# Weight preparation moved: transposes between the edge tables' counts, the experts' split beside the second feed-forward

## The reference, cut to what matters

```python
xn = layernorm(x)
x = x + gcn(xn, W, edges) + mix0(xn)             # message sum over the edges; attention mixer; feed-forward 0
x = x + experts0(layernorm(x))                   # 8 experts
xn = layernorm(x)
x = x + attention(xn, src, dst, Wq, Wk, Wv, Wp)  # edge softmax, then: h = layernorm(...)
                                                 # h = gelu(h @ W1.T + b1) @ W2.T + b2     (feed-forward 1)
    + ball_mixer(xn, w_qkv, w_dw, w_pw, w_res)   # convolution weights
x = x + shared(layernorm(x)) + top2_of_8(layernorm(x), W1p, W2p)
```

## Time and profile before

| what | value |
|---|---|
| median of 3 runs | 3988.4 us (3985.86 to 3989.91) |
| the profiled execution | 3987.43 us, span 3985.7 us |
| TensorE busy | 2587.3 us (65% of the span) |
| VectorE busy | 2170.5 us (54%) |
| ScalarE busy | 1269.1 us (32%) |
| GpSimd busy | 1315.5 us (33%) |
| mean granted TensorE clock | 0.807 |

### The profile page before, as it was taken

One profiled execution on the slowest core, in us unless ns is written; L12 is line 12 of the kernel. 1 busy time (PEld: TensorE's weight loads), 2 busy tenths in 40 slices (PEclk: granted clock), 3 DMA queues, 4 the chain that ended last, 5 costly groups with the idle time before them and its releaser, 6 DMA issues. The chain is left out here.

```text
span 3985.7 us, 66521 instructions
## 1 busy us (share of the span) xinstructions
PE 2587.3 (65%) x17122; PEld 2086.2 (52%) x17123; DVE 2170.5 (54%) x4408; ACT 1269.1 (32%) x2467; POOL 1315.5 (33%) x1017
## 2 busy tenths in 40 slices
PE   4413333436678699996375434777777487699997
PEld 4413333323367477774254423555555366589986
DVE  6523333322456388885237764777777555544445
ACT  0300010003143255553257732222222243345441
POOL 0048888853000000000001024888888500211115
PEclk9855555557679599997597767999999778699998
DMA  1046666730000000001200015777777200356643
GB/s 36 32 105 157 156 165 162 197 94 6 0 22 0 16 11 13 16 16 46 73 0 0 0 40 150 193 189 187 189 191 189 52 21 0 124 188 229 227 159 91
DMA packets 255391, 373.00 MB, mean 94 GB/s; under 512 B 119009, under 2 KB 180889, under 8 KB 250965
## 3 DMA queue, kind: packets, MB, share of 16 engines
q0 software_dynamic: 154752, 174.53, 18.2%
q1 hardware_dynamic: 87700, 185.50, 14.2%
q10 hardware_dynamic: 12864, 12.06, 1.1%
HBM read 320.09 MB, written 50.96 MB: 93 GB/s over the span
## 5 line engine op out<-in xcount | busy, mean ns | idle before, releaser
L750 POOL DMA_INDIRECT ms_got<-gather,ms_index x400 | 506.2, 1265 | 124.9 <-issue 114.4
L1689 POOL DMA_INDIRECT as_gkv<-gather_kv,as_index x340 | 462.0, 1359 | 108.7 <-issue 100.9
L811 PE MATMUL ms_total<-ms_got,ms_hot 125*125 125x256 f16 x1040 | 231.0, 410 | 376.8 <-DMA ms_got<-gather,ms_index 251.9
L811 PEld LDWEIGHTS ms_total<-ms_got,ms_hot 125*125 x1040 | 202.9, 219 | 405.0 <-issue 405.0
L2097 POOL MEMSET bm_fx<- 128x128 f32 x1 | 0.2, 205 | 1013.0 <-POOLq L115 1013.0
L1810 PE MATMUL as_total<-as_gkv,as_hot 125*125 125x264 f32 x850 | 218.8, 406 | 78.0 <-DVE as_summed L555 65.6
L1478 ACT ACTIVATE ex_h<-ex_up,ex_now 128x313 f32<-128x313 f32 (+1 forms) x320 | 196.1, 613 | 197.2 <-PE ex_up L458 190.0
L1810 PEld LDWEIGHTS as_total<-as_gkv,as_hot 125*125 125x125 f32 x850 | 157.7, 193 | 117.8 <-issue 91.8
L2791 DVE CAST moe_hidden<-moe_h 128x256 f16<-128x256 f32 (+1 forms) x336 | 101.8, 303 | 209.9 <-ACT moe_h L2728 209.3
L2728 ACT ACTIVATE moe_h<-moe_up,moe_w 128x256 f32<-128x256 f32 (+1 forms) x336 | 163.1, 487 | 135.2 <-PE moe_up L458 93.2
L1784 PE MATMUL as_picked<-y_rows,as_pick 125*125 x1060 | 150.3, 291 | 52.6 <-issue 47.7
(11 more groups left out here) (448 smaller groups left out, 5895.2 us busy)
## 6 DMA issues: line engine op xcount, KB each, us to landing
moe_w<-wsplit SPq DMA_DIRECT2D x34, 2052.0 KB
as_dsts<-in_dst SPq DMA_DIRECT2D x83, 305.2 KB
wsplit<-ms_split SPq DMA_DIRECT2D x36, 512.0 KB
ms_raw<-in_L_ffn_W1p SPq DMA_DIRECT2D x16, 512.0 KB
ms_raw<-in_L_ffn_W2p SPq DMA_DIRECT2D x16, 512.0 KB
results<-moe_made SPq DMA_DIRECT2D x32, 256.0 KB, 8.2
ms_got<-gather,ms_index POOLq DMA_INDIRECT x400
gather_kv<-qkv_out SPq DMA_DIRECT2D x5, 1250.0 KB
```

Source lines behind the costliest of these rows:

```text
L750: pool.indirect_dma_start(out=got[:, s, j, :], out_offset=None, in_=m.gather0, in_offset=bass.IndirectOffsetOnAxis(ap=index[:, s, j:j + 1] ...
L811: ins = pe.matmul(total[:, visit % RING, 0:C], hot[:, visit % RING, j, :], got[:, s, j, p * C:(p + 1) * C], start=(j + p == 0), stop=(j + ...
L1689: pool.indirect_dma_start(out=gkv[s][:, j, 0:2 * C], out_offset=None, in_=m.gather_kv, in_offset=bass.IndirectOffsetOnAxis(ap=index[:, s, ...
```

## The change

`Turner` is moved in front of `edge_tables` and used there: its 26 blocks are spread over the 20 steps of the counts, which are written out instead of looped, and ScalarE's loads, copies and stores stand before its one square root. The `Splitter` is used in `feed_forward("ff1")`, with four steps in each of the first four chunks and two in the last; its `high` stand on ScalarE behind gelu 3 and 11 and, twice, behind gelu 15; its `low` on VectorE behind units 7 and 15 and behind additions 2 and 4. The message sum keeps neither. `feed_forward` loses the code for more than one expert, which no call used. The core of the diff:

```diff
 def edge_tables(nc, m, a, src, dst):
...
+        turner = Turner(nc, m, a, ph)
...
             @block.scalar
             def _(act):
+                for i in range(2):
+                    turner.load(act, i)
+                turner.store(act)
                 act.wait_ge(s_span, 2)
                 act.activation(m.degree_s[:, 0, :], m.degree_s[:, 0, :], ACT.Sqrt).then_inc(s_rows, 1)
+                turner.finish(act)
...
+                steps, blocks = ET // SET, len(turner.blocks)
+                for i in range(steps):
+                    pe.wait_ge(s_hot, i + 1)
+                    add(i % 2, i == 0, i == steps - 1)
+                    turner.turn(pe, range(blocks * i // steps, blocks * (i + 1) // steps))
...
 def message_sum(nc, m, a):
...
-        turner = Turner(nc, m, a, ph)
-        splitter = Splitter(nc, m, a, ph)
...
-                        if splits and s % 2:
-                            splitter.low(dve, i, s // 2)
...
-                    turner.turn(pe, part, PARTS)
...
+def feed_forward(nc, m, a, name, W1, b1, W2, gain, bias_in, splits=False):
+    PIECES = 4
...
+                if splits:
+                    with sp.Fori(0, X8) as e:
+                        for h in range(2):
+                            splitter.move(sp, e, h)
+                    for h in range(2):
+                        splitter.move(sp, X8, h)
+                    splitter.finish(sp)
...
+                def highs(c, own, k):
+                    if splits and (own or k < 2):
+                        for s in range(2):
+                            splitter.high(act, c * PIECES + k, s)
+                def chunk(c, own):
+                    for u in range(units):
...
+                        act.activation(h32[:, u % 4, 0:n], up[:, u % 4, 0:n], ACT.Gelu,
+                                       scale=1.0 / WS, bias=bias[:, f:f + 1]).then_inc(s_h32, 1)
+                        if u % 8 == 3:
+                            highs(c, own, u // 8)
+                    highs(c, own, 2)
+                    highs(c, own, 3)
...
+                def chunk(c, own):
+                    for u in range(units):
...
+                        if u % 8 == 7:
+                            lows(c, own, u // 8)
+                    for j in range(J):
...
+                        if j in (2, 4):
+                            lows(c, own, 1 + j // 2)
```

More of the change, by code:

```diff
@@ L565, in finish @@
         self.dve.sem_inc(s_pace, 1)
[L568 to L625, removed]
@@ L762, in _ @@
                 adder = Adder(nc, dve, "ms", m.x, total, s_total, s_added, m.inv_sqrt_degree)
-                def groups(i, splits):
+                with dve.Fori(0, G // SLOTS) as i:
                     for s in range(SLOTS):
@@ L784, in groups @@
                         dve.tensor_copy(index[:, free, :], nxt).then_inc(s_index, 1)
-                        if splits and s % 2:
-                            splitter.low(dve, i, s // 2)
-                    return before + count
-                with dve.Fori(0, whole) as i:
-                    groups(i, True)
-                with dve.Fori(whole, G // SLOTS) as i:
-                    visits = groups(i, False)
-                adder.finish(dve.snap(visits), s_pace)
+                adder.finish(dve.snap(before + count), s_pace)
             @block.tensor
@@ L906, in feed_forward, with part, every_chunk @@
             ph.sem(x) for x in ("up", "h32", "hhigh", "hidden", "down", "added"))
-        ph.ahead(s_h32, s_hidden, s_down, s_added)
+        splitter = Splitter(nc, m, a, ph) if splits else None
+        if splits:
+            splitter.s_pace = s_pace
+        ph.ahead(s_hidden, s_down, s_added, s_h32)
         units = FB * len(HALVES)
         w1_32 = w[:, 0:CB * F].rearrange("p (b n) -> p b n", b=CB)
-        def part(s, k, layer, b, at, n):
+        def part(k, layer, b, at, n):
             start = b * F + at if layer == 0 else CB * F + b * C + at
-            return w16[:, s, k, start:start + n]
+            return w16[:, k, start:start + n]
+        def every_chunk(eng, work):
+            with eng.Fori(0, CHUNKS - 1) as c:
+                work(c, True)
+            work(CHUNKS - 1, False)
         with nc.Block() as block:
@@ L919, in _ @@
             def _(sp):
[L920 to L933 removed]
+                sp.dma_start(w1_32, W1.rearrange("(b p) n -> p b n", p=128)).then_inc(s_w, 16)
@@ L1008, in _ @@
+                every_chunk(act, chunk)
             @block.vector
             def _(dve):
[L1010 to L1012 removed]
+                dve.tensor_scalar(gain_s[:, :], gain, WS, None, ALU.mult).then_inc(s_gain, 1)
+                dve.wait_ge(s_gain, 1)
                 dve.wait_ge(s_high, 1)
[L1014 to L1023 removed]
@@ L1059, in mixer0 @@
+                every_chunk(dve, chunk)
 def mixer0(nc, m, a):
```

321 lines of the change are left out of this document (134 added, 187 removed).

## The result

Medians of this comparison: before 3987.1 us (3982.97 to 3989.91, 4 runs), after **4081.8 us** (4075.32 to 4092.51, 4 runs). Ratio 1.0241, 95% interval 1.0216 to 1.0266. The forecast was 4058 with 4028 to 4105: the direction, the range and the mechanism hold, the size is 24 us short. The profiled execution of after took 4075.32 us (span 4073.6) against 3987.43 for the one before: +87.9, and the stages are compared on these two.

A forecast was written before the change was run, and what follows sets the result against it. No engine was taken to bound the whole span, so each stage was read for itself. Message sum -24.2, edge tables +9 and second feed-forward +86.6 made +71.4 on 3987.4 us: 4058 us, range 4028 to 4105.

The forecast's parts named there:

- Rival 1: Second feed-forward: the cover holds, only VectorE's late splits show, up to 8 us; program 3980 us; chance 0.02.
- R: Second feed-forward: round trip from a step's second low half through store and loads to the next high, 6.6 us (5.1 to 10.9).
- the line through both gives ... 6.4 us for 1.5 MB: Second feed-forward: R's transfer time from two load rows without gathers, 0.25 MB in 2.59 us and 2 MB in 7.92.
- The estimate from the Trainium skill: Second feed-forward: a DMA as 2.0 us plus bytes at 436 GB/s, 5.6 of the 6.4 us, program 14 us lower.
- the message sum: Gathers freed of splits, 10 us, and six turner blocks gone behind the last group, 14.2 us: sum -24.2 us.
- Each split paid in full: Message sum: all 36 splits (44.1 us) locking GpSimd out for their whole length would put the program 33 us lower.
- GpSimd's idle is issue alone: Message sum: so the turner's other four parts, which delay TensorE in mid-stage, are worth nothing.
- the edge tables: Counts taking in the turner: step 13 +2.3, conv loads +1.5, small waits +2, tail +3.2; sum +9 us (+4 to +30).
- under 1 us and inside that landing: Edge tables' tail: square root behind the last store's issue, VectorE's last steps behind it, hidden in the store's landing.
- Rival 2: Second feed-forward: TensorE's clock falls to 1.2 GHz in the pauses, +28 us, program 4087 us; chance 0.15.
- Rivals 3 to 5: 3: turner bound by loads, +30, chance 0.12; 4: R as beside gathers, 10.9, +73, 0.08; 5: gathers gain nothing, +10.

The follow-up runs named there:

- Experiment 3: The change with two sets of raw and split buffers in the second feed-forward, each step's loads issued ahead of the previous step's stores: 3999.5 us, ratio 1.0045.
- turner_earlier: Kernel before with the turner in the edge tables, first loads held until edges are cast, blocks turned earlier, Sqrt of one number issued early: 3979.3 us, ratio 0.9987.
- stores_twice: The change with every splitter store issued a second time, to a tensor that nothing reads: 4163.5 us, ratio 1.0446.
- experiment 8: The change with 28 more matmuls, results overwritten, at two places of each chunk where TensorE waits: 4088.1 us, ratio 1.0253.
- experiment 4: turner_earlier with the 18 split steps spread over both feed-forwards, two per chunk, raw and split buffers twice: 4004.8 us, ratio 1.0045.
- Experiment 5: experiment 4 with both steps of a chunk moved beside the second layer's products: 3966.5 us, ratio 0.9957 to the kernel before.

## Why the prediction was right, and what was sized wrongly

**Right, the mechanism.** The splitter's chain of waits was named as what costs, with 17 round trips that nothing overlaps. Experiment 3 takes the chain away and leaves all the work: 83.6 of 105.9 us go. Rival 1 (the cover holds) is out: a chunk took 50 us, and it would have needed R at 1.75 or less.

**Wrong, the size of R.** The step that failed is "the line through both gives ... 6.4 us for 1.5 MB". R measured 7.8 on average (6.9 to 8.7), in the quoted chunk 7.9: 17 x (7.9 - 6.6) = 22 us, where the stage was 19.3 us above forecast. Two things are missing in that step, and both are in the trace of after. The first load was issued 0.9 us behind the second low half on average (1.1 in the quoted round trip), as SyncE issues the stores first; the step adds 0.17 for the way to the store and nothing for the loads' place behind it. And 1.5 MB is not all that was on the queue: the store of the first piece was issued about 1 us before the second low half ended, and a store took 4.2 us to land (median; 2.8 to 6.2), so it was still under way. How the missing 1.2 us divide between these two and the slope of the line (3.05 us per MB, from two rows of loads alone) stays open. Stores and loads together moved 273 GB/s where the engines were nearly full, 3.8 us per MB; the fixed part of the line and SyncE's 0.17 (2.0 us together) and 1.5 MB at that rate would make 7.8, an estimate that meets the measured R, but with 1.5 MB and no late issue, so its agreement proves little. The estimate from the Trainium skill ("DMA: Bandwidth & Descriptors", anatomy of one DMA), which stood beside it, was 14 us lower still, so the measurement lies further from it than from the row's line; the page gives that fit for DMAs that GpSimd issues, and these are SyncE's.

**Right, the message sum.** Forecast -24.2, in this pair of profiles -27.3. Over the nine other kernels with neither helper the stage takes 624.4 to 630.9 us, on average 627.7; with the splitter alone it takes 641.1 and 639.4. So the turner is worth 651.5 - 640.3 = 11.2 us (forecast 14.2) and the splits 640.3 - 627.7 = 12.6 (forecast 10). Each is off by 3 us, which is what executions of the same stage differ by here. Each split paid in full, as the prediction read the rule of the two separate sides (the Trainium skill, "SBUF — State Buffer"), would have taken 33 us more off; no such gain is in any run. The gathers still lengthen, 494.0 - 400 x 1.209 = 10.4 us in all, and nearly all of it in the 49 gathers that begin within a one-hot tile, which stayed. It was 20.6, so the gathers' own gain was 10.2, as forecast. "GpSimd's idle is issue alone" was not quite so: the earlier trace rows has 114.4 us of issue and some 10 of waits for VectorE's index copies, and they stayed too (110.9 and 14).

**Right in size, wrong about the tail's chain: the edge tables.** +10.6 against +9. The last count ended 6.9 us later (114.70, was 107.84; forecast 5.8) and the tail behind it took 3.7 more (7.3, was 3.5; forecast 3.2). The counts took the transposes in, with small waits for `conv` loads as foreseen. The sentence that failed is that the square root is "under 1 us and inside that landing": a table load of 1.28 us stands before it, and the chain over it (copies, table, square root, two steps of VectorE) ended the stage: 2.08 us from its last instruction to the next stage, as where no store is left over. The turner's first loads also ran beside the edges' own, and VectorE's first cast began 1.1 us later (33.07, was 31.94); with those loads held back (turner_earlier) it began at 31.60.

**Rival 2, the clock.** Its fact came true and its price did not. The granted clock was 0.77 to 0.84 in the chunks in place of 1.00, as the rule in the Trainium skill says of pauses ("TensorE: Matmul & The Clock Gate", HAM oscillation). But the chain outside R did not grow: from a step's second high half to its second low half it took 6.87 us beside first products (forecast 7.24, at the full clock) and 2.43 beside second ones (forecast 2.29), in every one of the 17 steps, and the same in stores_twice at a granted clock of 0.70 to 0.76. So TensorE was slow where it would have waited anyway. The direct test of experiment 8 settled nothing, since the filler matmuls hardly brought the clock back. The price is not nothing everywhere: in experiment 4, where TensorE waits little, it is part of the 5.9 us. (The rival's own terms, 4 x 4.2 + 10.5, add to 27 and not to 28.)

**Rivals 3 to 5.** The turner is not bound by its loads (+10.6, not +30). R is not what it is beside gathers (7.9, not 10.9). The gathers did gain.

What stays open: how much of R each missing part makes, why R differs by 1.3 us between the first and the second step of an expert, and how much of the 22 us in experiment 3 is the transfers' rate. Experiment 5 shows that at half the density next to nothing of it is left once the steps stand beside the second product.

## What to carry to other kernels

Background work that is copied in, worked on by two engines in order and stored again costs its round trip once per step wherever its host stage is in lock-step, however idle the host's engines are on average: give it a second set of buffers before moving it. Then place it by the host's phase, not by its mean load: nine steps cost some 3.6 us each in the phase in which VectorE had 0.81 us of work per 0.81 us, and next to nothing in the phase in which it waited for TensorE. Time a round trip from rows that store and load together, and count every issue on the queue ahead of the load that is waited for: a line through loads alone was 1.2 us short of 7.8, seventeen times.

## What the runs showed that I had not expected

- With a `Copy` on ScalarE ahead of it, a `Sqrt` got a table load of 1.28 us at the end of a stage, though the load for it had stood at the start before; a Sqrt of one number issued earlier hid it.
- One more megabyte of stores lengthened a round trip by 4.7 us, 1.4 of it because two more issues stood in front of the loads, while SyncE's order of loads and stores was worth 0.1.
- With the clock down to 0.77 to 0.84 the change lost nothing that its waits did not already cost; in experiment 4 waits of some 2 us in a chunk let one tile take 4.25 us in place of 2.62.
- TensorE was busy 26.00 of 26.00 us at the full clock beside transfers of 162 GB/s, which didn't disturb it.
- A wait of ScalarE of 11.65 us in the second product of a chunk cost TensorE only 2.4 us, as it had four units of the next chunk to make meanwhile.
